# An attention and feed-forward layer on one Trainium2 core: four rows laid over the partitions by matmul, and the opening and the drain in another order

## The chip, the cores and the metric

The kernel runs on one core of one Trainium2 chip. The metric is the device time of one execution in microseconds (us), taken as the median of several runs. The core's engines run side by side and meet at semaphores only: TensorE (PE) for matmuls and transposes, VectorE (DVE), ScalarE (ACT), GpSimd (POOL) and SyncE (SP), which issues most DMA transfers.

## The reference

The layer has a gated cross attention and a gated feed-forward part, over 32 batches of 128 rows of 512 numbers, all in fp32. Only the image half of the attention is needed: the context has 128 rows, fewer than the 257 that count as image, so the text half is empty.

```python
xn = layernorm(x)
q = rms_norm(xn @ q_w.T + q_b) * norm_q_w          # 16 heads of 32
k = rms_norm(ctx @ k_img_w.T + k_img_b) * norm_k_img_w
v = ctx @ v_img_w.T + v_img_b
x = x + tanh(g_xattn) * (softmax(q k^T / sqrt(32)) v @ o_w.T + o_b)
h = layernorm(x)
y = square(relu(h @ up_w)) @ down_w + (h @ expert_weight) * sum(top2(h @ gate_w))
out = x + tanh(g_ffn) * (layernorm(y) * ln_gamma + ln_beta)
```

## The kernel before

Each engine has a program written out by hand, in order; the order of the calls in `before`, `opening`, `slot` and `drain` is the order in which the engine works. An engine that waits for a semaphore holds up everything behind it. `run` calls `before()`, then slots -1 to 2, then a loop over the middle slots, then the last slots and `drain` for batches 30 and 31. Slots -1 and 0 are taken by `opening`. Slot s computes the scores and exponentials of batch s, and prepares batch n = s + 1 (K, Q and V products) and the x and context tiles behind it; a = s - 1 is the batch whose probabilities are turned and multiplied by V.

A product keeps fp32 accuracy by three fast matmuls: each operand is split into a rounded part (hi, by ScalarE's `copy`) and the rest (lo, by VectorE or GpSimd), and `mm3` (L76 to L78) multiplies hi by hi, hi by lo, lo by hi. So before a product of 12 matmuls (four slices k) can run, its weights (`weight_hi`, `weight_lo`), its context tile (`hi_ctx`, `lo_ctx`) and its x tile (`hi_xT`, `lo_xT`) must be split. The weights wk, wq, wv, wo are numbered 0 to 3; x and context come from tiles `xin` and `cin`, and the split tiles lie in `eight`. K goes to bank 6, is biased by VectorE into kb, squared by ScalarE, its scale rk comes from GpSimd (`inv_rms_k`), VectorE's `scale_k` makes kf, PE turns kf and ScalarE copies it to kT. Q goes the same way with qb, rq, qf (by ScalarE's `scale_q`) and qT. `inv_std` gives the scale of layernorm, `normalise` applies it to xn, which PE turns (`turn_x`). `keep_clock` issues matmuls whose result nobody reads.

Four vectors of 512 numbers (biases bk and bq, norm weights nq and nk) are wanted on all 128 partitions. `row` loads each by a DMA that reads the row 128 times; VectorE multiplies nq and nk into nqk.

After the last scores the drain mixes the last batches with the start of the feed-forward part: `ff.turn`, `ff.hi_T` and `ff.lo_T` turn and split its first eight tiles in PSUM banks given by T_BANK; `up_hi`, `up_lo` and GpSimd's `up_sums` prepare, for each of eight quarters q, three pieces m of the upward weights and sums of them; `upward` multiplies a quarter by seven products (a Strassen-like scheme: `sum_2`, `sums_all`), `squares` squares the result, and `downward` (L76 to L78 on the tile wide) multiplies it down. `gate` is L1662, its copy by ScalarE is lg (L1734), turned by PE at L1670.

## Time and profile before

| | |
|---|---|
| median of 3 runs | 1321.38 us (1320.49 to 1322.36) |
| profiled execution, its own time | 1320.95 us |
| its span, first to last instruction | 1318.7 us |
| PE busy | 1285.2 us, 97% |
| VectorE, ScalarE, GpSimd busy | 72%, 44%, 39% |
| mean granted PE clock | 0.996 of full |

The time of the profiled execution is a little more than its span, since something lies around the first and last instruction. Busy shares are those of instructions that overlap; an engine that is busy all the time can still run at half its clock.

### The profile page before, as it was taken

To read this page: it belongs to the slowest core of one execution; us is meant where nothing else is said; L and a number is where in the kernel's file an instruction comes from. 1 tells how busy PE (TensorE), PEld (TensorE's weight loads), DVE (VectorE), ACT (ScalarE), POOL (GpSimd) and SP (SyncE) were. 2 spreads that over 40 slices of the span, in tenths; PEclk is the share of its full clock that TensorE was granted. 3 is DMA by queue.
4 is the path that set the end of the run, shared out by engine and by line. 5 is a ranking of instruction groups with operands and counts; after the bars stand their busy time and mean duration, and the time that the engine had idled before them with its cause. 6 is when DMAs were issued, how large, how long until landed. Compare 5 with 4: busy or idle time off the path is not lost.

```text
span 1318.7 us, 28658 instructions
## 1 busy us (share of the span) xinstructions
PE 1285.2 (97%) x9316; PEld 1112.7 (84%) x9316; DVE 955.8 (72%) x1823; ACT 582.2 (44%) x1834; POOL 517.6 (39%) x672
## 2 busy tenths in 40 slices
PE   6999999999999999999999999999999999999997
PEld 4788888888888887888988988888998898888886
DVE  4677777777777776895776776776776776776765
ACT  4777777777777776333113123123222222212221
POOL 2566666666657774450240240240240240240121
PEclk9999999999999999999999999999999999999999
DMA  6289888888988863549368368368368368367542
GB/s 241 81 202 222 225 226 233 227 223 219 233 205 200 205 145 93 193 123 270 132 168 245 130 171 250 120 175 247 122 183 249 111 183 250 110 182 227 175 132 64
DMA packets 403580, 243.75 MB, mean 185 GB/s; under 512 B 303928, under 2 KB 304056, under 8 KB 403512
## 3 DMA queue, kind: packets, MB, share of 16 engines
q1 hardware_dynamic: 370872, 183.63, 52.9%
q10 hardware_dynamic: 32640, 59.26, 13.4%
q8 instruction: 37, 0.61, 0.2%
q14 instruction: 31, 0.25, 0.1%
HBM read 178.60 MB, written 64.23 MB: 184 GB/s over the span
## 4 chain that ended last, share of the span: by engine, by line
PE 76%; issue 9%; DVE 7%; POOL 2%; DMA 1%; ACT 1%; ACTq 0%; DVEq 0%; POOLq 0%; SPq 0%
PE bank L76 16%; PE bank L78 16%; PE bank L77 15%; PE wide L76 6%; PE wide L77 6%; PE wide L78 6%; PE bank L406 4%; PE wide L394 3%; PE bank L415 2%; DMA pair<-x_scratch 1%; PE wide L1662 1%; DVE c L1467 1%; POOL yrstd L1961 1%; DVE yst L1840 1%; DVE up_lo L1348 1%
## 5 line engine op out<-in xcount | busy, mean ns | idle before, releaser
L1734 ACT ACTIVATE hT_hi<-c 128x512 fp32r<-128x512 f32 x128 | 79.8, 632 | 397.6 <-PE wide L78 205.1
L1968 POOL TENSOR_TENSOR pair<-pair,beta 128x512 f32<-128x512 f32 x28 | 37.8, 1350 | 443.6 <-DMA pair<-x_scratch 443.6
L76 PE MATMUL wide<-wo_hi,hT_hi 128*128 128x512 f32 x512 | 200.4, 391 | 1.0 <-DVE route L1824 1.0
L77 PE MATMUL wide<-wo_lo,hT_hi 128*128 128x512 f32 x512 | 200.1, 391 | 0.0
L78 PE MATMUL wide<-wo_hi,hT_lo 128*128 128x512 f32 x512 | 199.5, 390 | 0.0
L782 ACT ACTIVATE prob<-wide,nmx 128x128 f32<-128x128 f32 x512 | 182.1, 411 | 2.5 <-DVE nmx L595 2.5
L957 POOL TENSOR_TENSOR prob<-prob,rr 128x512 f32<-128x512 f32 x128 | 132.6, 1040 | 84.2 <-DVE rr L603 84.2
L1814 DVE TENSOR_TENSOR hT_lo<-c,hT_hi 128x512 fp32r<-128x512 f32 x128 | 97.3, 781 | 67.1 <-ACT hT_hi L1734 67.0
L782 ACT ACTIVATION_READ_ACCUMULATOR prob<-wide,nmx 128x1 f32 x512 | 129.0, 252 | 0.0
L76 PEld LDWEIGHTS wide<-wo_hi,hT_hi 128*128 128x128 f32 x512 | 96.1, 188 | 21.1 <-issue 2.2
L78 PEld LDWEIGHTS wide<-wo_hi,hT_lo 128*128 128x128 f32 x512 | 96.2, 188 | 20.8
L76 PE MATMUL bank<-wq_hi,up_hi 128*128 128x256 f32 x384 | 108.8, 283 | 4.4 <-DVE c L1440 4.3
L77 PEld LDWEIGHTS wide<-wo_lo,hT_hi 128*128 128x128 f32 x512 | 96.1, 188 | 17.8
L78 PE MATMUL bank<-wq_hi,up_lo 128*128 128x256 f32 x384 | 109.3, 285 | 0.0
L77 PE MATMUL bank<-wq_lo,up_hi 128*128 128x256 f32 x384 | 109.0, 284 | 0.0
L595 DVE TENSOR_REDUCE nmx<-wide 128x4 f32<-128x512 f32 x128 | 82.1, 682 | 13.1 <-PE wide L394 13.1
L1467 DVE SCALAR_TENSOR_TENSOR c<-c 128x512 f32<-128x512 f32 x128 | 85.1, 705 | 0.0
L76 PE MATMUL bank<-wv_hi,up_hi 128*128 128x256 f32 x288 | 81.5, 283 | 0.8 <-DVE c L1461 0.8
L78 PE MATMUL bank<-wv_hi,up_lo 128*128 128x256 f32 x288 | 82.0, 285 | 0.0
L77 PE MATMUL bank<-wv_lo,up_hi 128*128 128x256 f32 x288 | 81.7, 284 | 0.0
L756 ACT ACTIVATE pT<-bank 128x512 f32<-128x512 f32 x122 | 66.0, 597 | 33.8 <-PE bank L406 33.8
L76 PEld LDWEIGHTS bank<-wq_hi,up_hi 128*128 128x128 f32 x384 | 72.9, 190 | 6.1 <-DVE c L1440 6.1
(233 smaller groups left out, 3484.7 us busy)
## 6 DMA issues: line engine op xcount, KB each, us to landing
wo_hi<-ring_scratch ACTq DMA_DIRECT2D x110, 256.0 KB, 3.6
wo_lo<-ring_scratch ACTq DMA_DIRECT2D x110, 256.0 KB, 4.5
wo_hi<-ring_scratch SPq DMA_DIRECT2D x46, 256.0 KB, 2.8
wo_lo<-ring_scratch SPq DMA_DIRECT2D x46, 256.0 KB, 3.0
xin<-in_x SPq DMA_DIRECT2D x32, 256.0 KB, 3.9
cin<-in_ctxT SPq DMA_DIRECT2D x32, 256.0 KB, 3.3
xres<-in_x SPq DMA_DIRECT2D x32, 256.0 KB, 3.9
x_scratch<-x SPq DMA_DIRECT2D x32, 256.0 KB, 3.5
```

The costliest lines, as they stand in the source:

```text
L76: eng.matmul(dst, ah, bh, start=first and k == 0, stop=False)
L77: eng.matmul(dst, ah, bl, start=False, stop=False)
L78: mm = eng.matmul(dst, al, bh, start=False, stop=last and k == n - 1)
L394: mm = pe.matmul(cols(bank[g], h), cols(qT, h)[strip(g), :], cols(kT, h)[strip(g)], start=True, stop=True)
L406: mm = pe.transpose(cols(btp(a, g), h), prob[par][:, g, h * P:(h + 1) * P], ident[:, :])
L595: dve.tensor_reduce(nmx[:, g * HG:(g + 1) * HG], bank[g].rearrange("p (h k) -> p h k", h=HG), AX.X, ALU.max, negate=True).then_inc(dv_mx, 1)
L756: return act.activation(dst, src, ACT.Copy)
L782: i = act.activation(prob[par][:, g, h * P:(h + 1) * P], cols(bank[g], h), ACT.Exp, bias=nmx[:, n:n + 1], scale=1.0, accum_out=rs[:, n:n + 1])
L957: pool.tensor_tensor(p, p, r, ALU.mult).then_inc(po_p, 1)
L1467: dve.scalar_tensor_tensor(out=cc[:, m, :], in0=cc[:, m, :], scalar=0.0, in1=cc[:, m, :], op0=ALU.max, op1=ALU.mult).then_inc(dv_h, 1)
L1734: return act.activation(dst, src, ACT.Copy)
L1814: dve.tensor_tensor(ff.hT_lo[i % 2][:, :], ff.c[i // 2 % 2][:, i % 2, :], ff.hT_hi[i % 2][:, :].bitcast(F32), ALU.subtract).then_inc(ff.dv ...
```

## The change

Five things are changed. **The rows:** ScalarE loads nq, nk, bk and bq as one row each, on one partition, into tiles that are not used yet; GpSimd multiplies nq by nk there; PE multiplies each of three rows by a row of ones, which lays it over 128 partitions in a PSUM bank; ScalarE copies it out. SyncE loads ident behind wk. **The first batch:** ScalarE splits all of wk before x, VectorE too; qb comes before kf; GpSimd does rk, rq, then inv_std; fewer `keep_clock` matmuls. **The second batch (slot 0):** ScalarE puts its last group of exponentials behind the context and x copies, GpSimd its context split ahead of two divisions, and VectorE's four wo splits and the scaling of tgbo go into slot 1. SyncE gets a wait there, since the first load of the feed-forward part overwrites the stage of wo. **The drain:** PE turns in another order and through other banks, VectorE's inverse of batch 31 comes earlier, residual_sum later. **The feed-forward start:** VectorE does `up_lo(1, 2)` before `sums_all`.

```diff
--- before.py
+++ after.py
@@ rows @@
+            first_rows = [(n, a[0:1, :]) for n, a in zip(("nq", "nk", "bk", "bq"), (k_dealt, q_dealt, x_dealt, x_turned))]
+            one_row = qf[0:1, 0:P]
@@ sync: before(), slot() @@
                     load(0, 0, t["x"], xin, ld_x)
-                    sp.dma_start(ident[:, :], t["ident"]).then_inc(s_ident, DMA)
                     load(0, 0, t["ctxT"], cin, ld_c)
                     weight(0)
+                    sp.dma_start(ident[:, :], t["ident"]).then_inc(s_ident, DMA)
...
+                    if is_slot(s, 1):
+                        sp.wait_ge(wl, 2 * KT + KT // 2 + KT)
                     if ff.has_half(s - 1):
                         ff.q_load(sp, s - 1, 1 - par)
@@ tensor: before(), opening(), drain() @@
                 def before():
+                    pe.wait_ge(s_pow, 2)
+                    pe.wait_ge(ld_rows, len(first_rows) * DMA)
+                    for n, (_, a) in enumerate(first_rows[2:] + first_rows[:1]):
+                        if n == 2:
+                            pe.wait_ge(po_nqk, 1)
+                        pe.matmul(bank[n], one_row, a, start=True, stop=True).then_inc(pe_rows, 1)
+                    pe.wait_ge(ac_c, 1)
+                    keep_clock(BV, 4, D)
                     pe.wait_ge(s_ident, DMA)
                     turn_x(0)
-                    pe.wait_ge(ac_c, 1)
-                    keep_clock(BV, 4, D)
...
-                        keep_clock(BV, 8, D)
+                        keep_clock(BV, 2, D)
...
                     ff.turn(pe, 2, t_first)
+                    pe.wait_ge(ac_e, s * NG + 1)
+                    ff.turn(pe, 3, t_first)
                     project_out(a, BO_NEXT)
...
+                    probs_taken(pe, s, 1)
+                    ff.turn(pe, 7, t_first)
+                    pe.wait_ge(ff.dv_T, 4)
                     values(s, s % 2)
-                    ff.turn(pe, 7, t_first)
@@ vector: opening(), slot() and drain() @@
-                    lo_xT(n)
                     if starting:
                         for k in range(1, KT):
                             weight_lo(0, k)
+                    lo_xT(n)
+                    if starting:
                         for k in range(KT):
                             weight_lo(1, k)
-                        dve.wait_ge(ld_bk, DMA)
+                        dve.wait_ge(ac_rows, 2)
                         add_bk(n)
-                        dve.wait_ge(ld_n, 2 * DMA)
-                        dve.tensor_tensor(as_strips(nqk[:, :]), by_strip(tgbo[:, :]), by_strip(junk_q[:, :]), ALU.mult).then_inc(cst, 1)
+                        add_bq(n)
                         dve.wait_ge(cst, 1)
-                        dve.wait_ge(ld_bq, DMA)
                         scale_k(n)
                         stats(1, 1)
-                        add_bq(n)
...
                     add_bk(n)
                     inverse(s, 1)
-                    inverse(s, 2)
                     add_bq(n)
                     scale_k(n)
+                    inverse(s, 2)
+                    normalise(n + 1, par)
+                    bias_v(n, 1 - par)
                     inverse(s, 3)
-                    normalise(n + 1, par)
                     stats(s + 3, 1 - par)
-                    bias_v(n, 1 - par)
-                    for k in range(KT):
-                        weight_lo(3, k)
...
+                    if is_slot(s, 1):
+                        dve.wait_ge(ld_bo, DMA)
+                        dve.wait_ge(s_tanh, 1)
+                        dve.tensor_scalar(tgbo[:, :], tgbo[:, :], tanh_g[:, 0:1], None, ALU.mult).then_inc(cst, 1)
+                        for k in range(KT // 2):
+                            weight_lo(3, k)
                     add_bq(n)
                     scale_k(n)
+                    if is_slot(s, 1):
+                        for k in range(KT // 2, KT):
+                            weight_lo(3, k)
...
                     maxima(s, 2)
+                    inverse(s, 0)
                     split_values(a)
+                    maxima(s, 3)
                     ff.lo_T(dve, 0, 0)
-                    maxima(s, 3)
-                    inverse(s, 0)
...
                     ff.up_lo(dve, 1, 0)
                     ff.up_lo(dve, 1, 1)
+                    ff.up_lo(dve, 1, 2)
                     ff.sums_all(dve, 0, 0)
-                    ff.up_lo(dve, 1, 2)
@@ scalar: before() @@
-                    row(act, bk, "bk", ld_bk)
-                    row(act, tgbo, "nq", ld_n)
-                    row(act, junk_q, "nk", ld_n)
-                    row(act, bq, "bq", ld_bq)
+                    for n, a in first_rows:
+                        act.dma_start(a, t[n]).then_inc(ld_rows, DMA)
                     hi_ctx(0, 0)
-                    weight_hi(0, 0)
+                    for n, dst in enumerate((bk, bq)):
+                        act.wait_ge(pe_rows, n + 1)
+                        copy(dst, bank[n]).then_inc(ac_rows, 1)
+                    act.wait_ge(pe_rows, 3)
+                    copy(as_strips(nqk[:, :]), by_strip(bank[2])).then_inc(cst, 1)
+                    for k in range(KT):
+                        weight_hi(0, k)
                     hi_xT(0)
-                    for k in range(1, KT):
-                        weight_hi(0, k)
@@ scalar: opening(), slot 0 @@
                     exps(s, par, 2)
-                    exps(s, par, 3)
                     square_q(n)
+                    hi_ctx(n + 1, par)
                     scale_q(n)
                     take_kT(n)
-                    hi_ctx(n + 1, par)
+                    hi_xT(n + 1)
+                    exps(s, par, 3)
                     take_qT(n)
-                    hi_xT(n + 1)
@@ gpsimd: before(), opening() @@
+                    pool.memset(one_row, 1.0).then_inc(s_pow, 1)
+                    pool.wait_ge(s_pow, 2)
+                    pool.wait_ge(ld_rows, len(first_rows) * DMA)
+                    nq, nk = first_rows[0][1], first_rows[1][1]
+                    pool.tensor_tensor(nq, nq, nk, ALU.mult).then_inc(po_nqk, 1)
...
                         inv_rms_k(0)
+                        inv_rms_q(0)
                         inv_std(1)
-                        inv_rms_q(0)
...
                     divide(s, par, 1)
+                    inv_rms_q(n)
+                    lo_ctx(n + 1, par)
                     divide(s, par, 2)
-                    inv_rms_q(n)
                     divide(s, par, 3)
-                    lo_ctx(n + 1, par)
@@ banks of the first turns @@
-    T_BANK = (6, 7, 5, 6, 7, 5, 7, 7)
+    T_BANK = (6, 7, 5, 0, 6, 5, 7, 2)
```

How ScalarE's instructions stand in the opening, up to the end of wq's splits, first in the kernel before (pair holds bk and bq, eight the split context and x, prob and fx the stages of wk and wq):

```order
L238 DMA pair<-in_bk 128x512
L238 DMA tgbo<-in_nq 128x512
L238 DMA junk_q<-in_nk 128x512
L238 DMA pair<-in_bq 128x512
L756 ACT_TABLE_LOAD
L756 ACTIVATE eight<-cin 128x512
L756 ACTIVATE wk_hi<-prob 128x512
L756 ACTIVATE eight<-bank 128x512
L756 ACTIVATE wk_hi<-prob 128x512 x3
L756 ACTIVATE wq_hi<-fx 128x512 x4
```

and in the changed kernel, where k_dealt, q_dealt, x_dealt and x_turned hold one row each:

```order
L807 DMA k_dealt<-in_nq 1x512
L807 DMA q_dealt<-in_nk 1x512
L807 DMA x_dealt<-in_bk 1x512
L807 DMA x_turned<-in_bq 1x512
L771 ACT_TABLE_LOAD
L771 ACTIVATE eight<-cin 128x512
L771 ACTIVATE pair<-wide 128x512 x2
L771 ACTIVATE nqk<-wide 128x512
L771 ACTIVATE wk_hi<-prob 128x512 x4
L771 ACTIVATE eight<-bank 128x512
L771 ACTIVATE wq_hi<-fx 128x512 x4
```

The loads shrink to one partition, three copies from PSUM (wide is banks 0 to 3) stand between the context copy and the first weight split, and the x copy moves behind wk.

How VectorE's instructions stand from the bias of V of batch 1 to the first maxima of batch 1, first before:

```order
L625 TENSOR_TENSOR vb<-bank,bv 128x512
L534 TENSOR_TENSOR wo_lo<-fx,wo_hi 128x512 x4
L678 TENSOR_SCALAR tgbo<-tgbo,tanh_g 128x512
L534 TENSOR_TENSOR eight<-bank,eight 128x512
L545 TENSOR_TENSOR kb<-bank,pair 128x512
L564 TENSOR_SCALAR xn<-xin,mv,rstd 128x512
L550 TENSOR_TENSOR qb<-bank,pair 128x512
L556 SCALAR_TENSOR_TENSOR kf<-kb,rk,nqk 128x512
L538 BN_STATS st<-xin 128x6
L541 BN_AGGR mv<-st 128x2
L595 TENSOR_REDUCE nmx<-wide 128x4 x3
```

and in the changed kernel:

```order
L554 BN_AGGR mv<-st 128x2
L547 TENSOR_TENSOR eight<-bank,eight 128x512
L558 TENSOR_TENSOR kb<-bank,pair 128x512
L577 TENSOR_SCALAR xn<-xin,mv,rstd 128x512
L702 TENSOR_SCALAR tgbo<-tgbo,tanh_g 128x512
L547 TENSOR_TENSOR wo_lo<-fx,wo_hi 128x512 x2
L563 TENSOR_TENSOR qb<-bank,pair 128x512
L569 SCALAR_TENSOR_TENSOR kf<-kb,rk,nqk 128x512
L547 TENSOR_TENSOR wo_lo<-fx,wo_hi 128x512 x2
L551 BN_STATS st<-xin 128x6
L554 BN_AGGR mv<-st 128x2
L608 TENSOR_REDUCE nmx<-wide 128x4 x3
```

The four wo splits and tgbo stood ahead of the x split (eight); now two and tgbo stand behind xn, two behind kf. The statistics (BN_STATS, BN_AGGR) of batch 3 now stand right ahead of the x split.

How VectorE's instructions stand at the start of the feed-forward part, from the last split of the drain (aT_lo) to the two squares, before:

```order
L534 TENSOR_TENSOR aT_lo<-wide,aT_hi 128x512
L1348 TENSOR_TENSOR eight<-fy,eight 128x512
L1348 TENSOR_TENSOR eight<-fy,eight 128x256
L1450 TENSOR_TENSOR c<-bank,c 128x256
L1452 TENSOR_TENSOR c<-bank,c 128x256
L1455 TENSOR_TENSOR c<-c 128x256
L1457 TENSOR_TENSOR c<-c 128x256
L1459 TENSOR_TENSOR c<-bank,c 128x256
L1461 TENSOR_TENSOR c<-c,bank 128x256
L1348 TENSOR_TENSOR eight<-pair,eight 128x1024
L614 SCALAR_TENSOR_TENSOR x_1<-wide,tanh_g,xres 128x512
L1467 SCALAR_TENSOR_TENSOR c<-c 128x512 x2
```

and in the changed kernel:

```order
L547 TENSOR_TENSOR aT_lo<-wide,aT_hi 128x512
L1368 TENSOR_TENSOR eight<-fy,eight 128x512
L1368 TENSOR_TENSOR eight<-fy,eight 128x256
L1368 TENSOR_TENSOR eight<-pair,eight 128x1024
L1470 TENSOR_TENSOR c<-bank,c 128x256
L1472 TENSOR_TENSOR c<-bank,c 128x256
L1475 TENSOR_TENSOR c<-c 128x256
L1477 TENSOR_TENSOR c<-c 128x256
L1479 TENSOR_TENSOR c<-bank,c 128x256
L1481 TENSOR_TENSOR c<-c,bank 128x256
L627 SCALAR_TENSOR_TENSOR x_1<-wide,tanh_g,xres 128x512
L1487 SCALAR_TENSOR_TENSOR c<-c 128x512 x2
```

The split `eight<-pair,eight` (up_lo of q = 1, m = 2) moved from behind the six sums of c to ahead of them.

## Rows read from the trace of the kernel before

**Rows 1.** The page's first part: busy us (share of the span) and instructions

```profile
PE 1285.2 (97%) x9316; PEld 1112.7 (84%) x9316; DVE 955.8 (72%) x1823; ACT 582.2 (44%) x1834; POOL 517.6 (39%) x672
```

**Rows 2.** What PE waited for, 0 to 62 us: total, times, longest us

```profile
PE bank L377 <- ACT qf L817: 1.8, 2, 1.4
PE bank L76 <- POOL eight L944: 1.7, 1, 1.7
PE bank L76 <- DVE eight L534: 1.1, 1, 1.1
```

**Rows 3.** The same, 499 to 548 us

```profile
PE wide L1670 <- ACT lg L1734: 2.2, 1, 2.2
...
PE wide L406 <- POOL prob L957: 0.8, 1, 0.8
PE bank L76 <- issue: 0.8, 1, 0.8
```

**Rows 4.** Timeline of ScalarE: start, length, engine, line, names [idle before]

```profile
2.12 0.45 ACTq L238 DMA_DIRECT2D pair<-in_bq  x1
...
10.70 0.63 ACT L756 ACTIVATE wk_hi<-prob 128x512 fp32r<-128x512 f32 x1 [0.80 <-DMA prob<-in_wk]
...
38.57 0.67 ACT L811 ACTIVATE junk_q<-qb 128x512 f32<-128x512 f32 x1
```

**Rows 5.** DMA issues up to 2.4 us: KB each, us to landing

```profile
pair<-in_bq ACTq DMA_DIRECT2D x1, 256.0 KB, 7.6
```

**Rows 6.** The page's DMA issues: KB each, median us to landing

```profile
wo_hi<-ring_scratch SPq DMA_DIRECT2D x46, 256.0 KB, 2.8
```

**Rows 7.** Windows, the gate's fp32 matmuls (L1662) alone

```profile
524.13:526.00 1.87, 1.87 (x64) 1.68 (x64) 1.00 0.87 291
```

**Rows 8.** Windows: length, busy of PE, PEld, DVE, ACT, POOL, granted clock, DMA

```profile
12.20:15.60 3.40, 3.40 (x8) 2.68 (x9) 3.40 (x7) 3.28 (x7) 0.00 (x0) 1.00 1.04 417
26.10:29.50 3.40, 3.40 (x8) 2.72 (x9) 2.05 (x4) 0.97 (x2) 2.10 (x3) 0.52 0.00 0
43.47:47.58 4.11, 3.02 (x13) 2.18 (x13) 3.56 (x7) 2.08 (x5) 0.78 (x2) 1.00 0.39 128
```

**Rows 9.** Timeline of VectorE in the opening

```profile
14.38 2.49 DVE L534 TENSOR_TENSOR wq_lo<-fx,wq_hi 128x512 fp32r<-128x512 f32 x4
...
19.46 0.75 DVE L556 SCALAR_TENSOR_TENSOR kf<-kb,rk,nqk 128x512 f32<-128x512 f32 x1 [1.22 <-POOL rk L935]
...
44.02 2.50 DVE L534 TENSOR_TENSOR wo_lo<-fx,wo_hi 128x512 fp32r<-128x512 f32 x4 [2.66 <-ACT wo_hi L756]
```

**Rows 10.** Timeline of PE in the opening

```profile
19.17 0.39 PE L78 MATMUL bank<-wq_hi,eight 128*128 128x512 f32 x1
...
26.10 0.80 PE L76 MATMUL bank<-wv_hi,eight 128*128 128x512 f32 x1 [0.43 <-POOL wv_lo L968]
...
30.31 1.17 PE L394 MATMUL wide<-kT,qT 32*128 32x128 f32 x32
...
36.77 0.39 PE L78 MATMUL bank<-wq_hi,eight 128*128 128x512 f32 x1
```

**Rows 11.** Timeline of GpSimd in the opening

```profile
23.38 2.67 POOL L968 TENSOR_TENSOR wv_lo<-fy,wv_hi 128x512 fp32r<-128x512 f32 x2
```

**Rows 12.** Chain of work up to 548 us: start, us, what

```profile
525.59 1.14 DVE eight L1348
...
527.39 1.94 DVE c L1467 x2
529.33 0.89 DVE gamma L1413
...
533.15 0.34 DVE c L1440
...
540.16 1.20 DVE c L1467 x2
```

**Rows 13.** What ScalarE waited for, 530 to 537 us

```profile
ACT up_hi L1335 <- DMA x_scratch<-x: 1.3, 1, 1.3
```

20 lines of the change are left out of this document (7 added, 13 removed).

## The prediction

> **What bounds the kernel now.** I read the busy times first: TensorE (PE) is busy for 97% of the span [rows 1], so a change can win only where PE stands still or runs slowly. The list of what PE waited for then shows where: in the first 62 us behind ScalarE's qf, behind GpSimd's split of the third context tile and behind VectorE's split of the third x tile [rows 2]; and at the passage into the feed-forward part behind ScalarE's copy lg, GpSimd's prob and an unnamed cause before an L76 [rows 3]. In the loop between the two, which the change leaves alone, PE has no waits. The result is thus a sum of three pieces, each followed up to an instruction of PE behind which nothing differs: A, the opening up to the scores of batch 0 at 30.31 us [rows 10]; B, from there to the Q product of batch 2 at 47.58; C, from the drain (499.6) to the L76 at 544.64.
>
> **A, removed and added.** Four loads of 256 KB, each one row read 128 times, leave ScalarE's queue: the last is issued at 2.12 and takes 7.6 us to land [rows 4, 5]. In their place come four loads of 2 KB, one GpSimd product on one partition, three fp32 matmuls of 512 columns from one partition, and three ScalarE copies that stand ahead of the first weight split. VectorE's product nqk goes, and ident is loaded behind wk. ScalarE's order shows the price: wk_hi began at 10.70 [rows 4]; now it can't begin before the third copy has ended. When do the rows land? The trace has no load so small. The quickest kind of 256 KB transfer takes 2.8 us [rows 6], which gives 4.9; the row issued last took 7.6 us, which gives 9.7. A 2 KB load competes with 2 MB of x, context and weights behind it on the other queue, but is nearer to the quick end: I take 5.0. The Trainium skill ("DMA: Bandwidth & Descriptors", on the two cost components) gives a fixed cost of about 2 us, by which they would land at 4.1 to 4.6 and the sum would be 0.4 us better; no run so far shows it. The matmuls: the gate's 64 fp32 records of 128 columns, which run four at a time over 32 columns each and two to an instruction, take 1.87 us in all [rows 7], so 8 times 0.23 us for 128 columns, 0.93 for 512, and 1.9 at the lower of the two clocks (1.2 GHz). At least they cost what a 512 column matmul costs at that clock, 0.43 (8 in 3.40 us with a granted 0.52 [rows 8]), at most 1.9. I take 1.8 each for three at the low clock, as PE is just starting: they end at 10.4. A copy takes 0.55, so the splits begin at 10.95, 0.25 later than before. GpSimd's product (1.3 us for such a row) lies beside the first two matmuls.
>
> **A, the chain behind.** VectorE then makes nine splits (wk, x, wq) of 0.62 us, the pace of the wq group [rows 9]: 0.65 after the first copy it starts, at 11.6, and ends at 17.1, against 16.9. The Q product ends one group of three matmuls later, about 17.9; in the trace its last matmul starts at 19.17 [rows 10], since PE did 8 matmuls of K in 3.40 us from 12.2 on [rows 8], the pace of the low clock. PE will have worked since 5.0 and should be at its high clock. But Q isn't on the path of K: kf began 2.6 us after the last of these splits, with kb, its squares and rk between them [rows 9]; again so, it begins at 19.7. What shortens the path is that qb now comes ahead of kf, so rq follows rk at once and is out of GpSimd's way. There inv_std(1) is followed by the two wv_lo splits, which before had to wait for rq until 23.38 [rows 11]. Now: kf ends at 20.3, the x statistics take 0.9 us and inv_std 0.85, so wv_lo starts at 22.05, 1.3 us earlier. V takes its second group after the second split, as before: 24.7 for 26.10 [rows 10]. PE's idle time is cut up (the fillers shrink from 8 to 2), in sum longer than before, so I keep the low clock that the trace shows under V, 9 matmuls at 0.43. **A gives 1.4 us.**
>
> The Trainium skill ("TensorE: Matmul & The Clock Gate", on what is actually happening) says that the throttled state is the default and that activity releases it, idleness brings it back. By that rule, the trace agrees: a granted 0.52 right after a stretch with waits [rows 8]. It leaves open whether V will be slow again. At 2.4 GHz throughout V, A would be 1.4 plus 9 times 0.2, or 3.2 us, against 1.4 at the low clock; this is a rival below.
>
> **B.** Times here are those of the trace, with scores(0) at 30.31 in both. Before, ScalarE began square_q at 38.57 [rows 4], behind the last group of exponentials; now that group comes behind it and behind the context copy, scale_q, take_kT and the x copy. Q ends at 37.0 [rows 10], qb at 37.7 and square_q at 38.4; the context copy ends at 39.0, rq at 39.4, and GpSimd's split, now ahead of two divisions, at 40.7. K of batch 2, which began at 43.47 behind 1.7 us of idleness [rows 2], can begin once qf is turned, 41.1. VectorE's wo splits (2.5 us) and tgbo (0.5) stood right ahead of the x split that let Q start at 47.58 [rows 8, 9]; they move into slot 1. The x split now waits for: last exponentials 41.3 to 42.7 (VectorE's inverse(3) stands ahead), statistics 0.9, split 0.65, so 44.4, and Q starts at 44.5, 0.6 after K ends. **B gives 3.1 us.** Where do the moved 3.0 us go? tgbo and two splits run while PE multiplies Q of batch 2 (2.7 us) after kb and xn, until 47.2, when qb is due; the other two end at 49.8, statistics 50.7. The scores of batch 1 end at 50.2, so the maxima are late by 0.5 us. ScalarE doesn't reach those exponentials before 52.4, so that is hidden; without this cover it costs 0.5. On SP the new wait for the fourth wo split stands ahead of one load into fx and of slot 2's xres; both were issued at 53 to 55, so the wait, over at 49.8, holds nothing up. What is late next is nothing on PE.
>
> **C.** In the drain rr of batch 31 comes before the last maxima, 1.8 us earlier, so the 0.8 us of waiting for prob [rows 3] goes, and the turns no longer wait for banks 6, 5 and 7 in turn. PE has fewer holes, but the values of batch 31 wait for VectorE's last take_probs, still about 514.3. Gained is the turn that stood behind them with its waits: the first product starts 0.8 us earlier. Then the big piece: up_lo(1,2), 1.14 us, stands on the chain at 525.59 [rows 12]; it now runs in VectorE's gap before the sums. That lets PE's q = 1 start without its 0.8 us of waiting [rows 3]; and it is what GpSimd's up_sums(2) waits for, which sends ScalarE's last part of up_hi and lg, and so PE's wait of 2.2 us [rows 3]. VectorE then is the bound up to sum_2 at 533.15 [rows 12]. Its chain loses 0.8 (drain), 1.14, and what GpSimd's up_sums beside it seem to cost: the two squares took 1.94 there and 1.20 later, so 0.74; gamma took 0.89 where I expect a half, so 0.4 [rows 12]. That is 3.1 us. Next late is a store: ScalarE's splits for q = 3 wait until x2 of the last batch has landed [rows 13], and that store, issued behind eight ring loads, moves by about 0.9 us only. VectorE reaches those splits 3.1 us earlier, waits, and is 2.2 us earlier at the sum before 544.64. **C gives 2.2 us**, bounds 0.8 (drain alone) and 3.1.
>
> **Sum.** 1.4 + 3.1 + 2.2 = 6.7 us. The profiled execution took 1320.95 us (span 1318.7); that is 0.43 under the median of 1321.38. The sum leads to 1314.25 from its own time and 1314.7 from the median. I predict 1314.4. With all low ends (rows landing at 9.7 turn A into -3.3; C 0.8; B 2.4, if Q of batch 2 gains no more than K does) it would be 1321; with all high ends (A 3.2 and 0.9 more if the clock rises during the three matmuls, C 3.1) 1310.8.
>
> **Rivals.**
> - *Warm V* (0.15): the high clock holds under V. For it: PE works from 5 us on instead of 8. Against: the idle pieces ahead of V sum to more than 3 us. A gives 3.2, the time is 1312.6.
> - *The rows are late* (0.12): they land near 7.5, the three matmuls and copies push wk_hi to 13.4, and A is -1.1. For: bq took 7.6 us. Against: its 256 KB are gone. 1316.9.
> - *The passage gives only the drain* (0.10): the store or a ring load sets the pace. C is 0.8: 1315.8.
> - *Slower: the low clock stays* (0.05): with shorter fillers it covers whole products. One of 12 matmuls at 0.43 for 0.23 costs 2.4 us; from three more low products than before on (7.2 us) the gain is gone, and with four (V of batch 0's last part, and K, Q and V of batch 1) the time is 1314.4 + 9.6, or 1324. Against it: in the trace the clock was back before the scores, and behind them PE is busy for 8 us.
> - *It does nothing it should* (0.03): within 0.2%, because another wait ends at the same instants: 1320.
>
> **How the numbers follow.** Likeliest is the sum, 0.55. 0.2% is 2.6 us, about what a measurement of this kernel can tell from no change. Late rows and a poor passage together still give 1318, so all but the last two rivals are faster: 0.91; within 0.2% 0.05, slower 0.04. The range takes in warm V with the full passage and late rows: 1311.6 to 1317.6.
>
> **What would show it.** In the changed profile: the three fp32 matmuls from about 5.0 at 1.8 us; wk_hi at 10.9; wv_lo at 22.0; scores(0) at 28.9; Q of batch 2 at 28.9 + 14.2 = 43.1; lg no longer waited for; sum_2 3.1 us nearer to the scores of batch 31; and at q = 2 of the feed-forward part a wait of PE of half a us or more. I am wrong if the first split starts after 12, if a granted clock near 0.5 stands anywhere behind the scores of batch 0, or if PE finds a new wait in slots 1 to 3 because of the 3 us that VectorE has more to do there.

## The result, and the profile after

The changed kernel took 1313.98 us (median of 6 runs, 1312.46 to 1316.5), against 1320.48 us (6 runs, 1319.83 to 1322.36) of the kernel before on the same chip: ratio 0.995, 95% interval 0.9938 to 0.9962. Forecast were 1314.4 us and a range of 1311.6 to 1317.6. The profiled execution took 1313.7 us, with a span of 1311.6, which is 7.1 less than before.

PE's busy time on the page is 1.1 us more than before [rows 1], so what has shrunk is the time in which it stood still:

```profile
PE 1286.3 (98%) x9316; PEld 1111.5 (85%) x9316; DVE 958.9 (73%) x1822; ACT 583.7 (45%) x1837; POOL 519.2 (40%) x674
```

What PE waited for in the first 62 us (total, times, longest us), to be held against [rows 2]:

```profile
PE wide L433 <- DMA x_turned<-in_bq: 4.8, 1, 4.8
PE bank L76 <- POOL wv_lo L988: 1.0, 2, 0.6
PE bank L381 <- ACT qf L834: 0.8, 1, 0.8
PE bank L76 <- DVE wv_lo L547: 0.6, 1, 0.6
```

and from 499 to 542 us, the passage into the feed-forward part, against [rows 3]:

```profile
PE bank L76 <- DVE c L1460: 1.6, 2, 1.0
PE bank L76 <- DVE c L1481: 0.5, 2, 0.3
PE wide L410 <- POOL prob L973: 0.4, 1, 0.4
```

The wait of 1.7 for GpSimd's context split is gone, and so is that of 2.2 for lg. New is PE's wait for VectorE's wv_lo in the opening. Its waits for sum_2 (L1460) were 0.4 in two and are 1.6 now: VectorE's chain shows through.

The timelines give the landmarks. GpSimd, ScalarE and PE in the opening (start, length, engine, line, operation; idle before and its releaser in brackets; an x behind the row counts instructions merged into it):

```profile
4.79 1.26 POOL L981 TENSOR_TENSOR k_dealt<-k_dealt,q_dealt 1x512 f32<-1x512 f32 x1 [3.83 <-DMA x_turned<-in_bq]
...
6.86 0.60 ACT L771 ACTIVATE pair<-wide 128x512 f32<-128x512 f32 x1 [2.05 <-PE wide L433]
8.57 0.60 ACT L771 ACTIVATE pair<-wide 128x512 f32<-128x512 f32 x1 [1.11 <-PE wide L433]
10.27 0.60 ACT L771 ACTIVATE nqk<-wide 128x512 f32<-128x512 f32 x1 [1.11 <-PE wide L433]
10.77 1.66 ACT L771 ACTIVATE wk_hi<-prob 128x512 fp32r<-128x512 f32 x3
...
22.28 2.70 POOL L988 TENSOR_TENSOR wv_lo<-fy,wv_hi 128x512 fp32r<-128x512 f32 x2
...
23.61 0.50 PE L76 MATMUL bank<-wv_hi,eight 128*128 128x512 f32 x1 [0.59 <-POOL wv_lo L988]
...
27.29 0.51 PE L76 MATMUL bank<-wv_hi,eight 128*128 128x512 f32 x1 [0.59 <-DVE wv_lo L547]
```

The copies stand 1.71 us apart: that is the pace of one row laid over the partitions. The last two rows are V's first matmul and the first of its last group. VectorE in the same stretch:

```profile
14.44 2.48 DVE L547 TENSOR_TENSOR wq_lo<-fx,wq_hi 128x512 fp32r<-128x512 f32 x4
...
19.00 0.69 DVE L563 TENSOR_TENSOR qb<-bank,pair 128x512 f32<-128x512 f32 x1 [1.47 <-PE bank L78]
19.61 0.74 DVE L569 SCALAR_TENSOR_TENSOR kf<-kb,rk,nqk 128x512 f32<-128x512 f32 x1
...
22.35 1.48 DVE L577 TENSOR_SCALAR xn<-xin,mv,rstd 128x512 f32<-128x512 f32 x1 [1.11 <-POOL rstd L951]
24.20 3.03 DVE L547 TENSOR_TENSOR wv_lo<-fy,wv_hi 128x512 fp32r<-128x512 f32 x2 [0.37 <-ACT wv_hi L771]
```

kf begins at 19.61, as forecast (19.7), but look at what is ahead of it: qb, which waited 1.47 us for Q. And the two wv_lo, 1.29 for two in the kernel before, take 3.03. At the passage (VectorE again) the first pair of squares, gamma, and the second and third sum_2:

```profile
521.50 1.28 DVE L1487 SCALAR_TENSOR_TENSOR c<-c 128x512 f32<-128x512 f32 x2
522.70 0.47 DVE L1433 TENSOR_SCALAR gamma<-gamma,tanh_g 128x512 f32<-128x512 f32 x1
...
525.56 0.41 DVE L1460 TENSOR_TENSOR c<-bank,c 128x256 f32<-128x256 f32 x1
...
537.42 0.41 DVE L1460 TENSOR_TENSOR c<-bank,c 128x256 f32<-128x256 f32 x1
```

**Where the 7.1 us went**, by landmarks of the two profiles: scores(0) at 28.63 for 30.31, 1.68 (piece A); from there to Q of batch 2 14.26 for 17.27, 3.01 (B); from that Q to the sum_2 at 537.42 (before: the last L1440, at 544.17) 494.53 for 496.59, 2.06 (C and the loop); the rest of the span 774.18 for 774.53, 0.35. In the 2.06 there is a loss: Q products of the loop follow each other every 15.10 us in both kernels, but near slot 6 two steps take 15.32 and 15.24, 0.36 more. So C is 2.4.

### The profile page after: what moved, and what is told of

Same layout as the page of the kernel before. It is cut to its first block, busy times and chain, and to the rows that moved or that the text cites. A ratio compares the mean times of both kernels' runs of the same rounds, so it can differ in the third digit from the quotient of the medians.

```text
span 1311.6 us, 28662 instructions
## 1 busy us (share of the span) xinstructions
PE 1286.3 (98%) x9316; PEld 1111.5 (85%) x9316; DVE 958.9 (73%) x1822; ACT 583.7 (45%) x1837; POOL 519.2 (40%) x674
## 3 DMA queue, kind: packets, MB, share of 16 engines
q10 hardware_dynamic: 32072, 58.22, 13.3%
## 4 chain that ended last, share of the span: by engine, by line
PE 75%; issue 11%; DVE 6%; DMA 2%; POOL 2%; ACT 1%; DVEq 0%; ACTq 0%; POOLq 0%; SPq 0%
PE bank L76 16%; PE bank L78 15%; PE bank L77 15%; PE wide L76 6%; PE wide L77 6%; PE wide L78 6%; PE bank L410 4%; PE wide L398 3%; PE bank L419 2%; PE wide L1682 1%; DVE c L1487 1%; POOL yrstd L1981 1%; DVE yst L1860 1%; POOL yvar L1979 1%; DMA x_scratch<-x 1%
## 5 line engine op out<-in xcount | busy, mean ns | idle before, releaser
L1988 POOL TENSOR_TENSOR pair<-pair,beta 128x512 f32<-128x512 f32 x28 | 39.5, 1410 | 443.9 <-DMA pair<-x_scratch 443.9
L1834 DVE TENSOR_TENSOR hT_lo<-c,hT_hi 128x512 fp32r<-128x512 f32 x128 | 100.1, 803 | 66.9 <-ACT hT_hi L1754 66.7
```

Of the source, the lines that this page charges most:

```text
L1834: dve.tensor_tensor(ff.hT_lo[i % 2][:, :], ff.c[i // 2 % 2][:, i % 2, :], ff.hT_hi[i % 2][:, :].bitcast(F32), ALU.subtract).then_inc(ff.dv ...
L1988: pool.tensor_tensor(res(g, j), res(g, j), ff.beta[:, :], ALU.add).then_inc(ff.po_r, 1)
```

## The experiments

One time tells little here: the median of the kernel before was 1322.08 us in the set of e1 to e4, 1320.23 in that of e5, e6, e9 and e10, and 1319.79 in that of e7 and e11 to e13 (each ratio is against its own set), and the stretch behind the last landmark, where all kernels have the same code, took 772.6 to 776.7 us in the profiles. So the landmarks decide. In the table, "Q" is the start of the last Q matmul of batch 0, "clock" the granted one under V of batch 0 ("low" where it fell for a stretch), "C" the time from Q of batch 2 to the last sum_2, and "loop" what its steps took over 15.10 each; all in us.

| kernel | time, median | ratio, 95% | Q | scores(0) | clock | B: to Q of batch 2 | C | loop |
|---|---|---|---|---|---|---|---|---|
| before | 1320.48 | | 19.17 | 30.31 | low | 17.27 | 496.59 | 0.0 |
| e13, before again | one run, 1318.49 | | 18.95 | 28.89 | high | 17.59 | 496.52 | 0.0 |
| changed | 1313.98 | 0.9938 to 0.9962 | 18.57 | 28.63 | high | 14.26 | 494.53 | 0.3 |
| e1 | 1315.4 | 0.9928 to 0.9973 | 18.96 | 29.48 | low | 14.28 | 496.63 | 0.3 |
| e2 | 1316.89 | 0.994 to 0.9971 | 20.49 | 30.69 | high | 14.26 | 494.63 | 0.9 |
| e3 | 1319.06 | 0.9957 to 0.9993 | 18.94 | 29.61 | low | 17.29 | 494.35 | 0.2 |
| e4 | 1317.23 | 0.9935 to 0.9967 | 18.29 | 28.34 | high | 14.30 | 496.17 | 0.6 |
| e5 | 1315.03 | 0.9939 to 0.9976 | 19.75 | 29.78 | high | 14.27 | 495.94 | 0.9 |
| e6 | 1313.76 | 0.9939 to 0.9972 | 18.10 | 28.13 | high | 14.27 | 494.28 | 0.5 |
| e7 | 1315.71 | 0.9958 to 0.9984 | 19.35 | 29.41 | high | 14.27 | 495.69 | 1.0 |
| e9 | 1316.03 | 0.9956 to 0.9983 | 20.16 | 30.83 | low | 14.27 | 494.55 | 0.3 |
| e10 | 1314.82 | 0.9947 to 0.9976 | 18.06 | 28.39 | high | 14.27 | 496.04 | 1.5 |
| e11 | 1311.36 | 0.9924 to 0.9962 | 18.97 | 27.37 | high | 14.27 | 494.08 | 0.2 |
| e12 | 1311.07 | 0.9931 to 0.997 | 18.25 | 26.64 | high | 14.27 | 494.44 | 0.6 |

**e3: the second batch (slot 0) in its old order.**

```diff
                     add_bk(n)
                     inverse(s, 1)
+                    inverse(s, 2)
                     add_bq(n)
                     scale_k(n)
-                    inverse(s, 2)
...
+                    for k in range(KT):
+                        weight_lo(3, k)
```

(and ScalarE's and GpSimd's part likewise.)

> The changed kernel with slot 0 of ScalarE, GpSimd and VectorE as before, with the four wo splits and tgbo at its end. Theory: Q of batch 2 starts 17.3 us behind the scores of batch 0, where the changed kernel has 14.3, and nothing gives it back: 3.0 us slower than the changed kernel, about 1317.0. Rival (part of the shift is absorbed in slots 1 to 3, where VectorE now has 3 us less to do): 1.5 to 2.5 us slower.

B went back to 17.29 (before: 17.27), and K of batch 2 to 13.18 behind scores(0) for 10.82. C stayed. So piece B is this reordering and nothing else, 3.0 us.

**e1: `up_lo(1, 2)` back behind `sums_all`. e4: the drain back in its old order.**

```diff
-                    ff.up_lo(dve, 1, 2)
                     ff.sums_all(dve, 0, 0)
+                    ff.up_lo(dve, 1, 2)
```

```diff
-    T_BANK = (6, 7, 5, 0, 6, 5, 7, 2)
+    T_BANK = (6, 7, 5, 6, 7, 5, 7, 7)
...
-                    inverse(s, 0)
                     split_values(a)
-                    maxima(s, 3)
                     ff.lo_T(dve, 0, 0)
+                    maxima(s, 3)
+                    inverse(s, 0)
```

> The changed kernel with up_lo of q = 1, m = 2 put back behind the six sums. Theory (VectorE's chain is the bound from the sums to sum_2): PE waits again about 0.8 us before the first product of q = 1 and about 2 us for lg; sum_2 of q = 1 ends about 2.3 us later against the drain's start; since the store of the last x2 is not moved, the x2-gated splits stand where they were, so that about 1.6 us are left at the end: about 1315.6 us where the changed kernel has 1314.0. Rival (the store alone sets the pace of the passage): less than 0.5 us at the end.

> The changed kernel with the drain of PE, VectorE and GpSimd and the banks of the first turns as before, but up_lo of q = 1, m = 2 still ahead of the sums. Theory: the first product starts 16.5 us behind the first probs of the drain, where the changed kernel has 15.65, and everything behind it, the ring loads and the store included, is 0.9 us later: about 1314.9. Rival (sum_2 and the store hide the drain's gain, since they are set by other waits): no difference, 1314.0.

e1 has C back at 496.63, and the wait for lg is there again (what PE waited for, 495 to 545 us):

```profile
PE wide L1690 <- ACT lg L1754: 2.2, 1, 2.2
```

C as a whole mixes this with other things, so take it apart at the three sum_2 that the passage has (start to start, us). The last column is from the issue of the last store, x2, to ScalarE's instruction that reads it back:

| kernel | Q of batch 31 to first sum_2 | first to second | second to third | store to reader |
|---|---|---|---|---|
| before | 31.50 | 15.14 | 11.10 | 7.56 |
| e13, before again | 31.51 | 15.16 | 11.11 | 7.67 |
| e1, up_lo back | 31.20 | 15.14 | 11.07 | 7.94 |
| e4, drain back | 31.50 | 12.82 | 12.31 | 8.26 |
| changed | 30.59 | 12.84 | 11.86 | 7.80 |
| e2, e3, e7, e9, e10, e11 | 30.59 to 30.63 | 12.82 to 12.84 | 11.36 to 12.34 | 7.31 to 8.27 |
| e5 | 31.23 | 12.83 | 12.10 | 8.04 |
| e6, e12, store first | 30.59, 30.61 | 12.83, 12.84 | 11.51, 11.53 | 7.46, 7.47 |

The drain's order is worth 0.9 us at the first sum_2. PE's first product of the feed-forward part starts as much earlier, 28.8 behind Q of batch 31 where e4 and the kernel before have 29.7. The move of `up_lo` is worth 2.3 between the first and the second. These two add up to the 3.2 us that lie between the kernel before and the changed one, and neither takes from the other. Behind the second sum_2 some of it is given back, 0.8 in the changed kernel and 0.3 to 1.2 in the others with the same passage, and this follows the last column: the later the stored rows can be read, the longer ScalarE and VectorE stand still. So C is 2.0 to 2.9 by the landing of one store, and the differences of C in the large table that are smaller than this are no effect of an edit. e1 and e5 lost 0.6 in the drain, where neither edit reaches; why is open. The move of the one 1.14 us instruction needs no more than its place.

**e2: the rows by DMA again, everything else changed. e9: the same, with PE busy from 1.5 us on.**

```diff
-                    for n, (_, a) in enumerate(first_rows[2:] + first_rows[:1]):
-                        pe.matmul(bank[n], one_row, a, start=True, stop=True).then_inc(pe_rows, 1)
...
+                    row(act, bk, "bk", ld_bk)
+                    row(act, tgbo, "nq", ld_n)
+                    row(act, junk_q, "nk", ld_n)
+                    row(act, bq, "bq", ld_bq)
```

e9 adds six such matmuls on a row of ones, whose result nobody reads, and has two fillers for four behind them:

```diff
+                    for n in range(6):
+                        pe.matmul(bank[n % 3], one_row, first_rows[0][1], start=True, stop=True)
```

> The changed kernel with the four rows again loaded by four transfers of 256 KB, VectorE's product nqk between kb and qb, and no row matmuls or copies; the new order of everything else stays. Theory of the prediction (the rows are near neutral, the new order of qb, rq and inv_std gives the gain of the opening): first weight split at 10.7, scores of batch 0 at 28.7 to 29.2 us, total within 0.6 us of the changed kernel. Rival (the gain comes from PE's early start, which has it at its high clock under K): K again at 0.43 us a matmul, scores of batch 0 at 29.7 to 30.3, total 1.1 to 1.7 us slower than the changed kernel.

> The rows come by broadcasting DMA again, as in e2_rows_by_dma, with the changed order of everything behind them, but TensorE is kept at work from its first cycles on: six 512-column fp32 matmuls on a row of ones, whose results nobody reads, stand before the transposes of x. Theory A (the opening gains because TensorE works early, so that K and Q of slot 0 run at the short pitch of 0.23 us instead of 0.43): K starts near 12.8 us, Q's last matmul ends before 19.3 (after: 18.8; e2: 20.9), kf is added by 20.2 and scores(0) starts at 28.4 to 29.6, where e2 had 30.69; the time is within 1 us of the changed kernel's, 1313.5 to 1315. Theory B (the broadcasting loads hold the weights' and the identity's loads back, or VectorE, whatever TensorE does): K and Q stay where e2 had them, scores(0) at 30.2 or later and the time 1315.5 or more. Which granted clock stands under V decides about 0.9 us of it, as it does between e1 and e4.

With the rows by DMA the rest of the change costs time: e2's scores(0) is at 30.69, above the ranges of both its theories, with the high clock under V, and at that level the kernel before has 28.89 (e13). Its ident, now issued behind wk, landed 9.2 us after issue, so PE waited for it until 12.04 where the kernel before turned x at 8.04. K began 0.4 later than in e13, and K's pace rose only at 17.95, where e13 has 15.06. (The granted clock of a window reads 1.00 under K in every profile, before too [rows 8], though K's matmuls stand 0.43 apart there. So up to 18 us the level is read from that pace, and "low clock under K" means no more.)

```profile
12.04 1.12 PE L381 MATMUL bank<-ident,xn 128*128 128x128 f32 x4 [2.18 <-DMA ident<-in_ident]
12.81 0.78 PE L76 MATMUL bank<-wk_hi,eight 128*128 128x512 f32 x1
...
17.65 0.46 PE L78 MATMUL bank<-wk_hi,eight 128*128 128x512 f32 x1
17.95 0.40 PE L76 MATMUL bank<-wq_hi,eight 128*128 128x512 f32 x1
```

In e9 PE did row matmuls from 1.48 to 12.09 without a hole and still met K at the low clock:

```profile
1.48 10.61 PE L430 MATMUL wide<-k_dealt,qf 1*128 1x512 f32 x12 [1.48 <-POOL k_dealt L976]
12.01 1.22 PE L425 MATMUL bank<-eight 128*128 128x512 f32 x2
13.03 1.06 PE L381 MATMUL bank<-ident,xn 128*128 128x128 f32 x4
13.74 0.78 PE L76 MATMUL bank<-wk_hi,eight 128*128 128x512 f32 x1
```

K's matmuls stand 0.43 apart until 16.0. Theory A (early work of PE makes K fast) falls: one-row fp32 matmuls, for 10.6 us, did not bring K to the short pace, and scores(0) came at 30.83. Theory B's price for the DMA rows stands, though e9 also starts K 0.9 later than e2, behind its own fillers.

**e10: the rows by matmul, the first batch in its old order.**

```diff
                         add_bk(n)
-                        add_bq(n)
                         dve.wait_ge(cst, 1)
                         scale_k(n)
                         stats(1, 1)
+                        add_bq(n)
...
-                        keep_clock(BV, 2, D)
+                        keep_clock(BV, 8, D)
```

(GpSimd's `inv_rms_q(0)` goes behind `inv_std(1)` again. ident's place and ScalarE's order stay as changed.)

> The rows by matmul as in the changed kernel, but the first batch in the order of before: VectorE adds bk to K and runs K's statistics before it adds bq, and GpSimd takes rk and the two factors before rq. Theory A (with TensorE early, Q comes so soon that the new order costs nothing and gains little): kf is added near 18.3, since it does not wait for Q, qb near 20, rq near 22, and scores(0) starts within 0.6 of the changed kernel's (28.3 to 29.6); the time is 1313.3 to 1315. Theory B (the new order is what brings the opening's gain): rq comes last and TensorE waits for the scaled Q, scores(0) at 30.2 or later and the time 1315.3 or more. A third outcome, scores(0) earlier than 28.2, would say that the new order costs time with the rows by matmul, since it puts kf behind Q.

Scores(0) at 28.39, where the changed opening at the high clock under V had 28.63, 28.34 and 28.13; behind the last Q matmul 10.33, where those had 10.03 to 10.06. So the new order of qb, rq and inv_std is worth 0.3 us at most. At the high clock under V the opening's account is thus: the kernel before 28.89, everything but the rows 30.69 (e2), with the rows 28.37, the mean of the three. The rows by matmul bring 2.3 us, and 1.8 of them only make up for what the rest of the change costs in e2, where ident is late and K's pace rises late. The rows alone, all else in the old order, were not run.

**e13: the kernel before, again. e7: six fillers for two ahead of the turned Q.**

```diff
-                        keep_clock(BV, 2, D)
+                        keep_clock(BV, 6, D)
```

> The kernel before, unchanged, for a second profile of its opening. Five executions of the changed kernel's opening had scores(0) at 28.13, 28.34 and 28.63 with V at the high granted clock and at 29.48 and 29.61 with V at the low one for a while. Theory A (the kernel before has the same two outcomes): scores(0) at 30.2 to 30.5 if V meets the low clock again, 28.7 to 29.5 if it doesn't, and then the opening's gain at equal clock is 0.6 to 0.9. Theory B (its first profile is what it always does): 30.2 to 30.5 whatever the granted clock under V.

> The changed kernel with six filler matmuls instead of two between the turning of K and the wait for the scaled Q. Before has eight there, the changed kernel two; e10 with eight had V at the high clock in one look. Theory A (the idle time of TensorE there is what lets the clock fall under V): V at the high clock, scores(0) at 28.0 to 28.7, time 1313 to 1314. Theory B (whether V meets the low clock is set otherwise, by when the clock rose under K: it rose at 13.3 to 13.8 where V was fast and at 14.9 and 15.0 where it was not): scores(0) follows K's rise and not the fillers, 28.1 to 28.7 with a rise before 13.9 and 29.4 to 29.7 with one after 14.8.

The second profile of the kernel before has scores(0) at 28.89, 1.42 us ahead of the first, with the same code. The windows of PE's busy time and granted clock from 24 to 28 us show why (length; busy of PE, PEld, DVE, ACT, POOL with counts; granted clock; DMA). In e13:

```profile
24.00:28.00 4.00, 3.29 (x15) 2.36 (x16) 1.89 (x3) 2.89 (x6) 2.79 (x3) 1.00 0.21 78
```

and of the changed opening, in e1:

```profile
24.00:28.00 4.00, 3.54 (x9) 2.60 (x10) 3.63 (x4) 1.59 (x4) 2.74 (x2) 0.62 0.21 70
```

Both levels occur in both kernels. Compared at one level the opening's gain is 28.89 less 28.37, 0.5 us at the high clock, and 30.31 less 29.55 (the mean of e1 and e3), 0.8 at the low one. e7's scores(0), at 29.41, fell on the number of theory B but not for its reason: V met the high clock, though K's pace rose as late as 15.9, and it was Q that came late (19.35). So theory B of that run falls; theory A is not shown either, since the kernel before has eight fillers and met both levels. What decides the level stays open.

In e13 the clock also fell under K of batch 2, behind PE's wait of 1.7 us for GpSimd's context split:

```profile
42.50:46.40 3.90, 3.90 (x12) 3.10 (x11) 3.49 (x6) 1.62 (x4) 0.44 (x1) 0.59 0.41 134
```

That is why its B is 0.3 longer. No profile with the changed slot 0 has that wait, and in all of them the granted clock from 31 to 62 us is 1.00.

**e11: wv's four remainders on VectorE alone.**

```diff
                         stats(1, 1)
+                        weight_lo(2, 0)
                         normalise(n + 1, par)
-                        for k in range(KT // 2, KT):
+                        for k in range(1, KT):
                             weight_lo(2, k)
... GpSimd
-                        weight_lo(2, 0)
-                        weight_lo(2, 1)
                         lo_ctx(1, 1)
```

> The changed kernel with all four remainders of wv taken by VectorE (the first ahead of x's next normalisation, the other three behind it) and none by GpSimd, which goes straight to the context block's remainder. In the changed kernel V began at 23.61 and then waited for VectorE's wv_lo(2): VectorE's two took 3.03 us beside GpSimd's two-input operations, where e10 has 1.29 for two. Theory A (V of the first slot waits for splits that the two engines stretch for each other, which gave back what the new order had brought): VectorE's four take 0.6 to 0.7 each, scores(0) starts 0.7 to 1.5 earlier than in the changed kernel at the same granted clock under V (26.8 to 27.9 at the high clock, where five executions of that opening had 28.1 to 28.6, and 28.0 to 28.9 at the low one), and the time is 1312.3 to 1313.5. Theory B (V's start or the clock holds scores(0), or the context's remainder on GpSimd now meets VectorE's splits instead): the splits still stretch to 1 us or more each, scores(0) at 28.1 to 29.6 and the time 1313.5 to 1315.

VectorE of e11:

```profile
21.55 0.66 DVE L545 TENSOR_TENSOR wv_lo<-fy,wv_hi 128x512 fp32r<-128x512 f32 x1
22.98 0.55 DVE L575 TENSOR_SCALAR xn<-xin,mv,rstd 128x512 f32<-128x512 f32 x1 [0.76 <-POOL rstd L950]
23.44 0.68 DVE L545 TENSOR_TENSOR wv_lo<-fy,wv_hi 128x512 fp32r<-128x512 f32 x1
24.60 1.29 DVE L545 TENSOR_TENSOR wv_lo<-fy,wv_hi 128x512 fp32r<-128x512 f32 x2 [0.47 <-ACT wv_hi L770]
```

The two last splits take 1.29 for 3.03, and xn 0.55 for 1.48, now that GpSimd does next to nothing beside them. From the last Q matmul to scores(0) it takes 8.40 us; the changed opening took 10.03 to 10.06 in four profiles at the high clock (changed, e4, e6, e7), and e13 9.94. So theory A holds in its number, 1.65 us, but only half of it is stretching. The start of V divides it:

| kernel | last Q matmul to V | V to scores(0) |
|---|---|---|
| e13, before again | 5.81 | 4.13 |
| e10, old first batch | 6.21 | 4.12 |
| changed | 5.04 | 5.02 |
| e11 | 4.20 | 4.20 |

The new order brought V 0.8 us nearer to Q than before, and V's second half gave back 0.9, since VectorE's splits now ran beside GpSimd's. e11 takes back these 0.8, and gains another 0.8 in front of V, since V no longer waits for GpSimd's first split, which takes 1.35 where VectorE's takes 0.66 and starts earlier. Only VectorE's splits were stretched: GpSimd's two took 2.70 beside them and 2.67 alone, before. The Trainium skill ("GPSIMD Engine Reference", on specifications) says that GpSimd shares its way to SBUF with VectorE, in contention with VectorE's two-input and two-port instructions. By that rule, the trace agrees: 0.64 against 1.52 us for one of VectorE's two-input splits.

**e6: the last store ahead of half the ring loads. e12: e6 and e11 together. e5: wk split earlier.**

```diff
-                    for n in range(KT):
+                    for n in range(KT // 2):
                         ff.ring_first(sp, n)
                     sp.wait_ge(dv_x2, s + 1)
                     sp.dma_start(in_rows(s, x2_dram[s]), x2[s % 2][:, :]).then_inc(st_x2[s % 2], DMA)
+                    for n in range(KT // 2, KT):
+                        ff.ring_first(sp, n)
```

> In the drain SyncE issues two of the four sets of next-ring loads, then the store of the last batch's half-normed rows, then the other two sets. In the changed kernel that store was issued at 521.61 and its rows were there for ScalarE at 529.41, 7.8 us later, behind the eight ring loads. Theory A (the store's landing is stretched by the ring loads that share the queue): it lands 2 to 4 us sooner, ScalarE's wait for x_scratch of 4.5 falls to under 2.5, sum_2 of the last slot comes 0.5 to 1.2 nearer to the drain's start (after: 42.1 behind its slot start) and the time falls by as much, to 1312.8 to 1313.5. Theory B (the landing is the store's own latency or the read's, or the ring loads set the next phase's start): no change at sum_2 of the last slot within 0.3, and the time 1313.5 to 1314.5, or slower where the next phase then waits for the ring.

In the changed kernel SyncE (queue, line, transfer) had been issuing ring loads up to the moment at which x2 was ready (residual_sum ended at 521.57):

```profile
521.12 0.44 SPq L1214 DMA_DIRECT2D wo_lo<-ring_scratch  x1
521.61 0.59 SPq L361 DMA_DIRECT2D x_scratch<-x  x1
522.29 2.39 SPq L1205 DMA_DIRECT2D fx<-x_scratch  x4
```

and in e6 the store goes out at 521.21, ScalarE goes on at 528.67:

```profile
521.21 0.59 SPq L361 DMA_DIRECT2D x_scratch<-x  x1
...
528.67 0.63 ACT L1357 ACTIVATE up_hi<-fy 128x512 fp32r<-128x512 f32 x1 [4.14 <-DMA x_scratch<-x]
```

That is 7.5 us for 7.8, with four ring loads ahead of it instead of eight. But with all eight ahead of it e2 has 7.3 and e11 7.5, so the 0.3 is within what the same code does. Theory B holds. The store had not waited for its queue but for its data, since it went out 39.5 us behind Q of batch 31 in both kernels, and what follows is a write and a read back.

> e11 and e6 together: wv's remainders on VectorE alone in the opening, and in the drain the store of the last half-normed rows ahead of the second half of the ring loads. If both work as each alone is supposed to and their gains add, scores(0) is where e11 has it and sum_2 of the last slot 51.8 to 52.1 us behind the drain's landmark (the changed kernel 52.56, e6 51.88), and the time is 1.4 to 2.2 below the changed kernel's: 1311.5 to 1312.6. If e11's theory B holds, only e6's 0.7 is left: 1313 to 1313.8.

Scores(0) at 26.64, 8.39 behind the last Q matmul as in e11. From Q of batch 31 to the third sum_2 it takes 54.98 us, where e11, without e6's edit, takes 55.01: the store's place adds nothing that can be seen. Against e4, whose Q ended at the same time (18.29), scores(0) is 1.70 earlier. The time, 1311.07 us, and e11's, 1311.36, are the lowest of all, but their intervals overlap that of the changed kernel; the landmarks show the gain in the opening, the times only do not contradict it.

For e5 ScalarE's part reads:

```diff
-                    for n, dst in enumerate((bk, bq)):
-                        act.wait_ge(pe_rows, n + 1)
-                        copy(dst, bank[n]).then_inc(ac_rows, 1)
-                    act.wait_ge(pe_rows, 3)
-                    copy(as_strips(nqk[:, :]), by_strip(bank[2])).then_inc(cst, 1)
-                    for k in range(KT):
-                        weight_hi(0, k)
+                    act.wait_ge(pe_rows, 1)
+                    copy(bk, bank[0]).then_inc(ac_rows, 1)
+                    for k in range(KT // 2):
+                        weight_hi(0, k)
```

(The copies of bq and nqk come later in its program; PE turns x ahead of the third row matmul, and its four fillers go.)

> In the opening ScalarE copies only bk out of PSUM before it rounds the first two slices of wk, bq between the second and the third, and the norm row last; TensorE turns x's first block before the third row matmul. In the changed kernel wk_hi started at 10.77 though wk's first slices had landed by about 8. Theory A (wk's rounding is what the opening waits for): wk_hi starts at 8.3 to 9.0, K at 11 to 12, and scores(0) 0.8 to 1.8 earlier than in the changed kernel at the same granted clock under V (26.8 to 27.8 at the high clock, 27.7 to 28.7 at the low one); the time 1312 to 1313.2. Theory B (x's turning, wq's landing or the row of bq, which qb and so kf need, holds Q and kf): wk_hi is earlier but Q's end is not by more than 0.4, scores(0) stays at 28.2 to 29.6, and the time at 1313.5 to 1315.

wk_hi began at 7.58 for 10.77, but K only at 12.16 for 12.75: the third row matmul now ended at 12.2, and K's pace rose only at 17.0. Scores(0) came at 29.78, just above theory B's range, with the high clock under V. So the copies in front of wk's splits are not what holds the opening; PE's rows, x's turn and K's pace are. Whether the missing fillers made the pace rise late is not shown.

## Why the prediction was right, and where it was not

The time was right, and of the three terms B and C were, with their mechanism. A came near its size in the two profiles only by errors that cancelled, and that part is luck.

**The rows.** Forecast landing 5.0, measured 4.78; three matmuls of 1.8, measured 1.71 from one to the next; end 10.4, measured about 10.2; wk_hi 10.95, measured 10.77; the ninth split ends at 17.1, measured 16.92. The bounds (9.7 for a slow landing) were far too wide.

**A, the chain behind.** Forecast 1.4; between the two profiles 1.68, but at equal clock 0.5 to 0.8. Three steps were off.
- "The Q product ends about 17.9": it ended at 18.96, since K began at the pace of the low clock in every profile (it rose at 13.3 to 15.9 us in the openings that are alike up to there). "PE will have worked since 5.0 and should be at its high clock" is the step that failed, and e9 shows that such matmuls don't bring that about. A second thing was left out: K began at 12.3 to 12.8, since four fillers and x's turn stand behind the third row matmul. Even with the earliest rise (e10) the Q product ended at 18.45.
- "But Q isn't on the path of K": with qb ahead of kf it is. kf fell on its forecast instant only because Q was ready then.
- The wv_lo splits did start earlier (22.28 for 23.38), but the sum took each at its old length. VectorE's two met GpSimd's work and took 3.03 for 1.29, and 0.9 of the gain went behind V's start. That is why e10 does nearly as well without the new order.

The prediction also took the high or low clock under K from the pace of its matmuls, 8 in 3.40 us, while the same row reads a granted clock of 1.00 [rows 8]; it did not say so.

What covered for this was the high clock under V in the profile of the changed kernel, where the low one was forecast, beside a low one in the profile of before. The rival of the warm V (0.15) thus came true in its condition, and not in its price: 3.2 forecast, 1.68 measured, because V's second half waited for VectorE instead (0.59 us in front of its last group).

**B.** Forecast 3.1, measured 3.0 (e3). K of batch 2 came at 10.82 behind scores(0), forecast 10.8; Q at 14.26, forecast 14.2. No wait of PE appeared in slots 1 to 3: the moved splits were hidden.

**C.** Forecast 0.8 at the first product, 3.1 at the second sum_2, then 2.2 behind the store. Measured 0.9, then 3.2 (43.43 us from Q of batch 31 for 46.64), then 2.4. The squares took 1.28 for the forecast 1.20 and gamma 0.47 where I expected a half. PE's wait before q = 1 fell from 0.8 to 0.2. What the sum didn't have is a wait of 1.03 at 526.03, inside q = 1, for its sum_2; VectorE's chain was the bound, so it cost nothing. The wait of half a us at q = 2 came as 0.52. The last step was right by its result only: the store was to move by 0.9 us and moved by 1.5 (39.5 behind Q of batch 31 for 41.0), and the 2.4 could as well have been 2.0 or 2.9, by the landing of that store.

**The sum.** 1.7 + 3.0 + 2.4 less 0.4 in the loop plus 0.35 behind it is 7.1 for 6.7. At equal clock under V the first term is 0.5 to 0.8, and the kernel gains about 6. The medians are 6.5 apart.

**Left open.** The loop's loss: all twelve profiles with some of the change have steps over 15.10 us, 0.2 to 1.5 in sum, at changing slots; the two profiles of before have none. In the changed kernel VectorE waited for the dealt k tile (k_dealt) 1.6 us in two waits near slot 6, before 0.7 in one, so a late transfer is possible. But from 100 to 460 us the two wait 5.1 us each for that tile, and e13 6.7 without a lost step. What makes the steps longer is not shown. Nor is what sets the clock's level under K and V.

## What to carry to other kernels

When a reorder lets a helper engine begin earlier, ask which instructions it now runs beside: a split that took 0.64 us alone took 1.52 beside another engine's, and that ate the 0.8 us that the earlier start had brought. Before crediting one part of a change with a difference between two profiles, look at the granted clock of that stretch in both; here it made 1.4 us in the same kernel. And in a passage where several waits end close together, find the short instruction that stands on the chain for no reason of data: moving one of 1.14 us was worth 2.3 at the next landmark. And before a difference of two profiles is put down to an edit, cut the stretch at landmarks and see how far each piece varies where the code is the same: here all pieces but the one behind a store agree within 0.1 us in most profiles.

## What the runs showed of the hardware

- A row laid over 128 partitions by an fp32 matmul of 512 columns from one partition took 1.71 us, and 10.6 us of such matmuls (e9: 12 records, 1.77 us for two) were followed by products at 0.43 us a matmul, the pace that goes with the low level (1.2 GHz) under V [rows 8]. No run has such a matmul at the high level.
- Four loads of 2 KB issued from 0.74 to 2.16 us had all landed at 4.78; the same rows as 256 KB broadcasts landed 4.2 to 8.6 us after their issue (e2), and ident, in the same place of its queue, took 9.2 there and 6.0 to 7.5 with the small loads.
- The same opening met V at the high granted clock in one execution and at 0.62 or 0.66 from 24 to 28 us in another. From the last Q matmul to scores(0) that is 10.03 to 10.06 against 10.52 and 10.67 in the changed kernel, and 9.94 against 11.14 in the one before.
- A one-input fp32 scaling of 512 columns on VectorE (xn) took 0.55 us alone and 1.48 to 1.62 beside GpSimd's two-input work; GpSimd's own splits were not stretched, 2.70 us for two against 2.67.
- A store of 128 rows to memory and its read back took 7.3 to 8.3 us from the store's issue to the reader's start, in fourteen profiles, and no less with four loads ahead of it (7.46, 7.47) than with eight (7.31 to 8.27).
